# Gated expert rows added straight to the output in memory, with the closing pass taken out

## The chip, the core and the metric

The kernel runs on one core of a Trainium2 chip. The core has five engines with a queue of instructions each: PE (TensorE, matrix products), DVE (VectorE), ACT (ScalarE), POOL (GpSimd) and SP (SyncE, which here only issues DMAs). They run side by side and wait for one another through semaphores. DMAs that SP issues and the indirect ones that POOL issues run on the same 16 DMA engines. The metric is the device time in microseconds (us); three runs of the kernel before took 547.4, 556.72 and 557.5 us (median 556.72).

## What is computed

Input: 16 batches of 256 tokens with 128 features, conditioning vectors `c` and weights. Cut to what matters:

```
mod = (silu(c) @ wmod).reshape(16, 6, 1, 128)       # sa, ca, ga, sb, cb, gb
ga, gb: sign kept, magnitude at least 0.25
x = x + ga * attention(layernorm(x) * (1 + ca) + sa)   # 16 heads, causal, clipped scores
h = layernorm(x) * (1 + cb) + sb
# feed-forward: each token goes to 2 of 8 experts
normed = rmsnorm(h) * norm_weight
w, idx = top_k(softmax(normed @ router), 2);  w = w / sum(w)
moe = sum over the 2 experts of w * (silu(normed @ Wg) * (normed @ Wu)) @ Wd
out = x + gb * (h + clip(alpha) * moe)
```

All data are float32.

## The kernel before

**Attention loop.** A software pipeline over the 16 batches (`schedule`, turns -3 to 18, two of them unrolled in a loop body). In turn i every engine runs its part (`emit`) for seven batches at once: `front` (projections) for batch i + 2, `attn` (scores, exponentials, clip) for i, `back` for i - 1, `norm` (second normalisation) for u = i - 2, `route` for q = i - 3, and so on. The order within a turn is written out by hand, engine by engine, and each engine runs its list strictly in that order.

SP's list in a turn: `load_bc` (modulation rows of batch i into `bc`, after POOL's residual add L1114 of batch i - 2, semaphore `base_ready`), `keys_out` and `queries_out` (L382 to L395: projected keys and queries of batch i + 2 to DRAM), then `stack` twice (L401: they come back stacked, four copies each, after the writes have landed). DVE's list: `route` first (ranks, the two gate weights L887 and L892, destinations L894 in the expert queues), then `clip` of the first scores (L863, L865), the normalised rows `h2` (L903), then the rest. ACT squares `h2` (L726), POOL takes the root and adds `h2` times a row to the residual in `xall` (L1114). After `route`, POOL scatters the rows in `pl` (128 normalised features, gate weight, row number: `PAYW` = 130 words) into the DRAM tensor `queue`, sorted by expert, by four indirect DMAs a batch (L1122).

**Change of stage.** DVE turns the counts into a table (`bi`): for each of 71 blocks of 128 rows its expert and its first row in `queue`. Blocks past the last one are dummies. SP pads the ends of the experts' queues (L425), reads table entries into registers (L431) and loads blocks into `xb`, 8 buffers (L437).

**Expert stage.** In `block_steps` PE transposes block n + 2 (L647), computes gate and up products of n + 1 (L640) and the down product of n - 1 (L654); ACT and DVE do the activation and product; DVE scales the result by the gate weight into `ysb`, 8 buffers (L1040). POOL scatters it to `ydram` (L1148), where each token has two rows of its own, so that no scatter touches another's rows. A buffer of `xb` is loaded again when its scatter has landed (`yscat`).

**Closing pass.** When all has landed, SP reads the two halves of `ydram` in 8 chunks (L460), DVE adds them (L1050) and multiplies by the modulation row `gb * alpha` (L1054), POOL adds the residual (L1157) and SP writes the output (L464).

## Time and profile before

| | us |
|---|---|
| runs (3) | 547.4, 556.72, 557.5 |
| profiled execution, its own time | 549.46 |
| its span, first to last instruction | 547.6 |
| PE busy / DVE / ACT / POOL | 403.5 / 312.4 / 269.0 / 252.6 |

The busy times overlap; they are sums over stages with different limits. The profile is of a single execution, whose time is 7 us under the median, so that a sum of durations from it stands against 549.46 and not against the median. Line numbers are those of the kernel before. In rows, `SPq` is SP issuing a DMA, `xN` a number of instructions, and what stands in brackets is the engine's idle time ahead of the row and what ended it.

### The profile page before, as it was taken

How to read it: one execution, taken by the hardware profiler on the slowest of the kernel's cores; microseconds unless marked ns; L12 is line 12 of the kernel's file. 1: busy time of each engine (PE TensorE's matmuls, PEld its weight loads, DVE VectorE, ACT ScalarE, POOL GpSimd, SP SyncE). 2: the span in 40 equal slices, each digit the busy share in tenths (PEclk: the TensorE clock that was granted, in tenths of full speed). 3: DMA queues.
4: the chain of work that ended last, by engine and by line, in shares of the span. 5: the costliest groups of instructions: out<-in, count | busy, mean ns of one | idle time of the engine just before them, and what ended most of it. 6: DMA issues, size and time to landing. Idle time of an engine off the chain costs nothing. (4 is left out here: it accounts for less than half of the span.)

```text
span 547.6 us, 12530 instructions
## 1 busy us (share of the span) xinstructions
PE 403.5 (74%) x3935; PEld 320.6 (59%) x3936; DVE 312.4 (57%) x976; ACT 269.0 (49%) x467; POOL 252.6 (46%) x306
## 2 busy tenths in 40 slices
PE   3568876976697697697678752199999999999400
PEld 1345554654464464465456432089999999999400
DVE  3428967667754755756666666235554554555284
ACT  1427755655555455456555542245656655565100
POOL 3103437435743643644573487314444444444453
PEclk9999978877966866868787775589999999999855
DMA  8367445445444434434543082332221122112194
GB/s 263 73 154 166 118 101 123 114 109 131 100 115 116 104 88 115 104 90 115 130 97 105 19 317 84 91 100 64 58 69 54 55 64 60 55 54 65 43 293 138
DMA packets 56002, 59.04 MB, mean 108 GB/s; under 512 B 7167, under 2 KB 48128, under 8 KB 55712
## 3 DMA queue, kind: packets, MB, share of 16 engines
q1 hardware_dynamic: 51648, 50.15, 35.3%
q0 software_dynamic: 4320, 8.47, 4.6%
q8 instruction: 18, 0.29, 0.2%
q14 instruction: 16, 0.13, 0.1%
HBM read 34.81 MB, written 24.23 MB: 108 GB/s over the span
## 5 line engine op out<-in xcount | busy, mean ns | idle before, releaser
L673 ACT ACTIVATE pt<-SC 128x1536 f32<-128x1536 f32 x64 | 92.8, 1451 | 103.5 <-PE SC L500 103.3
L863 DVE SCALAR_TENSOR_TENSOR pt<-pt,cst 128x1024 f32<-128x1024 f32 x64 | 79.6, 1243 | 64.8 <-ACT pt L673 64.7
L1148 POOL DMA_INDIRECT ydram<-ysb,xb x71 | 69.8, 982 | 97.6 <-DVE ysb L1040 96.3
L640 PE MATMUL SC<-xTs,wgu 128*128 128x128 f32 x852 | 110.1, 280 | 2.3 <-issue 1.3
L640 PEld LDWEIGHTS SC<-xTs,wgu 128*128 128x128 f32 x852 | 102.8, 195 | 4.1 <-issue 3.9
L500 PE MATMUL SC<-stq,stk 24*128 24x256 f32 (+1 forms) x1024 | 78.9, 435 | 10.9 <-DMA stq<-qdram 8.1
L1122 POOL DMA_INDIRECT queue<-pl,dest x64 | 77.7, 1215 | 18.0 <-issue 17.2
L500 PEld LDWEIGHTS SC<-stq,stk 24*128 24x128 f32 x1024 | 59.5, 240 | 28.6 <-DMA stq<-qdram 8.4
L777 ACT ACTIVATE wgu<-gu,ws 128x704 f32 x71 | 62.1, 875 | 19.5 <-issue 19.5
L522 PE MATMUL OB<-pt,va 128*32 128x256 f32 (+1 forms) x1024 | 68.1, 394 | 3.3 <-DVE pt L865 3.2
L784 ACT ACTIVATE sg<-SC 128x384 f32<-128x384 f32 x71 | 34.8, 490 | 59.6 <-PE SC L640 53.8
L1034 DVE TENSOR_TENSOR hidT<-sg,SC 128x384 f32<-128x384 f32 x71 | 39.3, 554 | 31.4 <-PE FB L654 16.0
L1104 POOL TENSOR_TENSOR gbh<-h,bc 128x128 f32<-128x128 f32 x32 | 15.1, 493 | 78.7 <-DVE h L903 78.7
L522 PEld LDWEIGHTS OB<-pt,va 128*32 128x32 f32 x1024 | 30.5, 126 | 33.4 <-issue 19.6
L532 PE MATMUL FB<-tot,ut_bf 128*128 128x8 bf16 x16 | 2.9, 183 | 58.5 <-DVE tot L976 58.5
L532 PEld LDWEIGHTS FB<-tot,ut_bf 128*128 128x128 bf16 x16 | 1.6, 99 | 62.4 <-DVE tot L976 62.4
L654 PE MATMUL FB<-dn,hidT 128*128 x216 | 30.1, 275 | 0.5 <-DVE ysb L1040 0.5
L865 DVE TENSOR_SCALAR pt<-pt 128x512 f32<-128x512 f32 x64 | 30.3, 474 | 0.0
L1070 POOL TENSOR_TENSOR rstd<-var,mhalf 128x8 f32<-128x8 f32 x4 | 8.4, 2103 | 47.0 <-DVE var L812 47.0
L910 DVE TENSOR_TENSOR rope<-FB,cst 76x512 f32<-76x512 f32 x16 | 11.0, 685 | 33.2 <-PE FB L561 33.2
L1029 DVE COPY xTs<-OB 128x128 f32<-128x128 f32 x36 | 10.5, 291 | 33.5 <-PE OB L647 33.5
L654 PE MATMUL BK<-dn,hidT 128*128 x210 | 29.3, 275 | 0.0
(150 smaller groups left out, 654.3 us busy)
## 6 DMA issues: line engine op xcount, KB each, us to landing
stk<-kdram SPq DMA_DIRECT2D x64, 96.0 KB
stq<-qdram SPq DMA_DIRECT2D x64, 96.0 KB
xb<-queue SPq DMA_DIRECT2D x71, 65.0 KB, 1.8
kdram<-rope SPq DMA_DIRECT2D x32, 128.0 KB
qdram<-rope SPq DMA_DIRECT2D x32, 128.0 KB, 3.8
bc<-modrow SPq DMA_DIRECT2D x16, 256.0 KB
pt<-ydram SPq DMA_DIRECT2D x16, 256.0 KB, 5.3
gu<-gup SPq DMA_DIRECT2D x1, 2816.0 KB, 12.1
```

Source lines behind the costliest of these rows:

```text
L500: last = mm(SC[:, i, kt * S:S + kt * P], stk[at_, par(a), j, kt * P:(kt + 1) * P], stq[at_, par(a), j, kt * P:S], start=True, stop=True)
L522: last = mm(OB[VW * i:VW * i + VW, g * S + kt * P:(g + 1) * S], va[:, par(a), kt, n * VW:(n + 1) * VW], pt[:, j, i, kt * S:S + kt * P], st ...
L640: last = mm(GUB[b[1] % 2][:, n, c * P:(c + 1) * P], wgu[:, b[1] % 2, n, c * P:(c + 1) * P], xTs[:, b[1] % 2, :], start=True, stop=True)
L654: last = mm(YP[b[1] % 2][:, 0:D], hidT[:, b[1] % 2, n * P:(n + 1) * P], dn[:, bass.ds(e * (3 * D) + n * D, D)], start=(n == 0), stop=(n == 2))
L673: af(pt[:, j, :, 0:S + P], SC[:, :, 0:S + P], ACT.Exp, scale=SCALE).then_inc(s["exp_done"], 1)
L777: af(wgu[:, b[1] % 2, :, 0:HID], gu[:, bass.ds(expert(b) * (2 * HID), 2 * HID)].rearrange("p (n h) -> p n h", n=2), ACT.Copy, scale=ws[:, ...
L784: af(sg[:, b[1] % 2, :], GUB[b[1] % 2][:, 0, 0:HW], ACT.Silu).then_inc(s["sg_ready"], 1)
L863: stt(out=diag, in0=diag, scalar=E_LO, in1=mask, op0=ALU.max, op1=ALU.min)
L865: ts(off, off, E_LO, E_HI, ALU.max, ALU.min).then_inc(s["clip_done"], 1)
L1034: tt(hidT[:, b[1] % 2, :], sg[:, b[1] % 2, :], GUB[b[1] % 2][:, 1, 0:HW], ALU.mult)\
L1122: G.indirect_dma_start(queue, bass.IndirectOffsetOnAxis(dest[:, par(q), 2 * t + k:2 * t + k + 1], 0), pl[:, par(q), t, k, :], None).then_i ...
L1148: G.indirect_dma_start(ydram, bass.IndirectOffsetOnAxis(xb[:, slot(b), D + 1:D + 2].bitcast(u32), 0), ysb[:, slot(b), :], None, bounds_che ...
```

## The change

Each expert row now carries its modulation row with it, and goes by an accumulating scatter straight to the row of its token in the output tensor.

- In the attention loop SP, at the end of its part of a turn, copies the modulation row of batch i - 2 next to the normalised rows in `pl` (`gate_rows`; rows become 258 words), and the residual rows of that batch to the output (`rows_out`). DVE's second gate value waits for the first of these copies.
- `queue` gets 8 dummy blocks, written at the start; POOL writes zeros to 128 spare rows behind the output.
- DVE multiplies by both gate weight and modulation row. It also writes, for each block, how far the scatters of the block before it and of the one two before it must have come: up to that one itself where the expert differs, else only up to that buffer's previous use.
- POOL reads these numbers into registers, 16 for eight blocks, waits for them and for the scatter three blocks back, and issues the scatter with an addition.
- The closing pass is gone. `xTs`, `sg`, `hidT` and `ysb` lie in the space of `pt`.

```diff
@@ -59,12 +59,12 @@
...
+XBUF = 8
-PAYW = D + 2
+PAYW = 2 * D + 2
...
@@ -97,8 +100,7 @@
...
-    queue = nc.dram_tensor("queue", [(DUMMY + 1) * P, PAYW], fp32).ap()
-    ydram = nc.dram_tensor("ydram", [2 * NTOK, D], fp32).ap()
+    queue = nc.dram_tensor("queue", [(DUMMY + XBUF) * P, PAYW], fp32).ap()
...
@@ -273,26 +274,25 @@
...
-        bi = sb("bi", [1, 2, NBLK], i32)
+        bi = sb("bi", [1, 4, NBLK], i32)
...
@@ -363,7 +363,10 @@
...
             sp.dma_start(modrow, mrow[:, :]).then_inc(s["modrow_out"], DMA)
             sp.wait_ge(s["cst_in"], DMA)
-            sp.dma_start(queue[DUMMY * P:(DUMMY + 1) * P, :], cst[:, C_PAD:C_PAD + PAYW]).then_inc(s["dummy_out"], DMA)
+            for n in range(XBUF):
+                sp.dma_start(queue[(DUMMY + n) * P:(DUMMY + n + 1) * P, :], cst[:, C_PAD:C_PAD + PAYW])\
+                  .then_inc(s["dummy_out"], DMA)
+            out_rows = out.rearrange("(n p) d -> p n d", p=P)
             sp.wait_ge(s["modrow_out"], DMA)
...
@@ -401,6 +404,18 @@
...
+            def rows_out(u):
+                need(sp, s["base_ready"], num(u) + 1)
+                sp.dma_start(out_rows[:, col(u, T), :],
+                             xall[:, xtile(u)].rearrange("p (t d) -> p t d", d=D)).then_inc(s["rows_out"], DMA)
+            def gate_rows(u):
+                need(sp, scat[par(u)], half(u) * (DMA * 4))
+                row = modrow[col(u), 4 * D:5 * D].rearrange("(o b) d -> o b d", o=1)
+                sp.dma_start(pl[:, par(u), :, :, D + 2:].rearrange("p t k d -> p (t k) d"),
+                             row.to_broadcast([P, 2 * T, D])).then_inc(gb_in[par(u)], DMA)
...
@@ -410,6 +425,15 @@
                     queries_out(f)
                     stack(kdram, stk, stk_in, "k_out", f)
                     stack(qdram, stq, stq_in, "q_out", f)
+                if peeled(i) == 1:
+                    sp.wait_ge(s["dummy_out"], XBUF * DMA)
+                    sp.dma_start(queue[DUMMY * P:(DUMMY + XBUF) * P, D + 1:D + 3].rearrange("(n p) o -> p n o", p=P),
+                                 cst[:, C_DID:C_DID + 2 * XBUF].rearrange("p (n o) -> p n o", o=2))\
+                      .then_inc(s["dummy_out"], DMA)
+                if norm:
+                    gate_rows(u)
+                    rows_out(u)
                 if peeled(i) == B - 1:
                     sp.dma_start(gu[:, :], gup).then_inc(s["w_in"], DMA)
                     sp.dma_start(dn[:, :], down).then_inc(s["w_in"], DMA)
@@ -429,42 +453,27 @@
...
                 _, rows = nc.values_load_multi_w_load_instructions(
-                    bi[0:1, 1, at], engines=[mybir.EngineType.SP], min_val=0, max_val=DUMMY * P)
+                    bi[0:1, 1, at], engines=[mybir.EngineType.SP], min_val=0, max_val=(DUMMY + XBUF - 1) * P)
...
                 for n, row in enumerate(rows):
                     b = plus(k, n)
-                    need(sp, yscat[slot(b)], uses(b) * DMA)
+                    need(sp, yscat[slot(b)], (uses(b) + 1) * DMA)
                     sp.dma_start(xb[:, slot(b), :], queue[bass.ds(row, P), :]).then_inc(xb_in[slot(b)], DMA)
...
-                sp.wait_ge(s["dummy_out"], DMA)
+                sp.wait_ge(s["dummy_out"], (XBUF + 1) * DMA)
                 sp.wait_ge(s["padded"], E * DMA)
...
             load((0, 0), UNR2, queues_written)
-            sp.wait_ge(s["pv_done"], 4 * B)
...
             with sp.Fori(1, M1) as m:
                 load((m, 0), UNR2)
             load((M1, 0), NBLK - M1 * UNR2)
             for n in range(XBUF):
-                sp.wait_ge(yscat[n], (NBLK - n + XBUF - 1) // XBUF * DMA)
...
+                sp.wait_ge(yscat[n], ((NBLK - n + XBUF - 1) // XBUF + 1) * DMA)
         @block.tensor
@@ -889,6 +898,7 @@
                     V.tensor_reduce(destf[:, :], pd[:, :, :, :].rearrange("p t k e -> p (t k) e"), AX.X, ALU.add)\
                         .then_inc(s["destf_ready"], 1)
                     need(dve, s["c0_ready"], num(q) + 1)
+                    need(dve, gb_in[par(q)], (half(q) + 1) * DMA)
                     tt(pl[:, par(q), :, 1, D], ex[:, par(q), :], pl[:, par(q), :, 0, D], ALU.mult)
                     need(dve, s["destf_ready"], num(q) + 1)
                     cp(dest[:, par(q), :], destf[:, :]).then_inc(s["dest_ready"], 1)
@@ -1014,11 +1024,20 @@
...
-            chain(ts(bf_[:, 2, :], bf_[:, 1, :], -1.0, float(DUMMY), ALU.mult, ALU.add))
+            chain(tt(bf_[:, 2, :], cst[0:1, C_DUM:C_DUM + NBLK], bf_[:, 1, :], ALU.subtract))
...
             ts(bi[:, 1, :], bf_[:, 1, :], float(P), None, ALU.mult).then_inc(s["table_ready"], 1)
+            V.memset(bh[:, 1:3, 0:2], 0.0)
+            chain(tt(bh[:, 0, :], bf_[:, 0, :], ge[:, :, NE1], ALU.add))
+            tt(bh[:, 1, 1:NBLK], bh[:, 0, 1:NBLK], bh[:, 0, 0:NBLK - 1], ALU.is_gt)
+            chain(tt(bh[:, 2, 2:NBLK], bh[:, 0, 2:NBLK], bh[:, 0, 0:NBLK - 2], ALU.is_gt))
+            for n in range(2):
+                stt(out=bi[:, 2 + n, :], in0=bh[:, 1 + n, :], scalar=float(DMA),
+                    in1=cst[0:1, C_USE + n * NBLK:C_USE + (n + 1) * NBLK], op0=ALU.mult, op1=ALU.add).then_inc(s["order_ready"], 1)
...
@@ -1036,23 +1055,12 @@
...
                     b = plus(k, -1)
                     need(dve, s["y_done"], nb_(b) + 1)
-                    need(dve, yscat[slot(b)], uses(b) * DMA)
-                    ts(ysb[:, slot(b), :], YP[b[1] % 2][:, 0:D], xb[:, slot(b), D:D + 1], None, ALU.mult)\
+                    need(dve, yscat[slot(b)], (uses(b) + 1) * DMA)
+                    stt(out=ysb[:, slot(b), :], in0=YP[b[1] % 2][:, 0:D], scalar=xb[:, slot(b), D:D + 1],
+                        in1=xb[:, slot(b), D + 2:2 * D + 2], op0=ALU.mult, op1=ALU.mult)\
                         .then_inc(s["y_ready"], 1)
             block_steps(dve, step)
-            dve.wait_ge(s["gba_in"], DMA)
...
         @block.gpsimd
@@ -1073,6 +1081,13 @@
...
             finish_stats(0)
+            pool.wait_ge(s["cst_in"], DMA)
+            for n in range(XBUF):
+                part = slice(n * (P // XBUF), (n + 1) * (P // XBUF))
+                pool.dma_start(out[NTOK + n * (P // XBUF):NTOK + (n + 1) * (P // XBUF), :], cst[part, C_PAD:C_PAD + D])\
+                    .then_inc(yscat[n], DMA)
...
@@ -1135,26 +1150,44 @@
             G = nc.gpsimd
-            below = G.to_reg(2 * NTOK - 2)
-            bound = pool.alloc_register("bound")
-            def step(k, x, g, d):
-                if not d:
-                    return
-                b = plus(k, -1)
+            pool.wait_ge(s["rows_out"], B * DMA)
+            below, bound = G.to_reg(NTOK + (XBUF + 1) * P - 2), pool.alloc_register("bound")
+            def landed(k, count):
+                at = slice(nb_(k), nb_(k) + count) if isinstance(k[0], int) else bass.ds(k[0] * UNR2, count)
+                counts = []
+                for n in range(2):
+                    apart(pool)
+                    _, row = nc.values_load_multi_w_load_instructions(
+                        bi[0:1, 2 + n, at], engines=[mybir.EngineType.Pool],
+                        min_val=DMA, max_val=DMA * (NBLK // XBUF + 2))
+                    counts.append(row)
+                return list(zip(*counts))
+            def add_rows(b, before):
+                in_loop = not isinstance(b[0], int)
                 need(pool, s["y_ready"], nb_(b) + 1)
+                if in_loop or nb_(b) >= 3:
+                    need(pool, yscat[slot(plus(b, -3))], (uses(plus(b, -3)) + 2) * DMA)
+                for n in range(2):
+                    if in_loop or nb_(b) >= n + 1:
+                        pool.wait_ge(yscat[slot(plus(b, -1 - n))], before[n])
                 pool.reg_add(bound, below, 1)
-                G.indirect_dma_start(ydram, bass.IndirectOffsetOnAxis(xb[:, slot(b), D + 1:D + 2].bitcast(u32), 0),
-                                     ysb[:, slot(b), :], None, bounds_check=bound, oob_is_err=False)\
+                G.indirect_dma_start(out, bass.IndirectOffsetOnAxis(xb[:, slot(b), D + 1:D + 2].bitcast(u32), 0),
+                                     ysb[:, slot(b), :], None, bounds_check=bound, compute_op=ALU.add)\
                  .then_inc(yscat[slot(b)], DMA)
-            block_steps(pool, step)
-            pool.wait_ge(s["base_ready"], B)
...
+            pool.wait_ge(s["order_ready"], 2)
+            for n, before in enumerate(landed((0, 0), UNR2)):
+                add_rows((0, n), before)
+            with pool.Fori(1, M1) as m:
+                for n, before in enumerate(landed((m, 0), UNR2)):
+                    add_rows((m, n), before)
+            for n, before in enumerate(landed((M1, 0), NBLK - M1 * UNR2)):
+                add_rows((0, M1 * UNR2 + n), before)
@@ -1179,9 +1212,15 @@
     for t in range(T):
         for k in range(2):
             for b in range(B):
-                c[:, C_IDS + 2 * (T * b + t) + k] = (k * NTOK + b * S + t * P + p).astype(np.int32).view(np.float32)
+                c[:, C_IDS + 2 * (T * b + t) + k] = (b * S + t * P + p).astype(np.int32).view(np.float32)
     c[:, C_BLK:C_BLK + NBLK] = np.arange(NBLK)
-    c[:, C_PAD + D + 1] = np.full(P, PADID, np.int32).view(np.float32)
+    for n in range(2):
+        c[:, C_USE + n * NBLK:C_USE + (n + 1) * NBLK] = \
+            (np.maximum(np.arange(NBLK) - 1 - n, 0) // XBUF + 1) * 16
...
@@ -1223,7 +1262,7 @@
...
-    out = nc.dram_tensor("out", (B, S, D), mybir.dt.float32, kind="ExternalOutput").ap()
+    out = nc.dram_tensor("out", (NTOK + (XBUF + 1) * P, D), mybir.dt.float32, kind="ExternalOutput").ap()
...
-    return r.results[0]["out"]
+    return r.results[0]["out"][0:NTOK].reshape(B, S, D)
```

The instruction streams show where this stands. SP, one turn of the loop, before (`L401` are the stack loads, `L372` the modulation rows of the next turn):

```order
L401 DMA stk<-kdram 24x1024 [waits k_out]
L401 DMA stk<-kdram 24x1024 x3
L401 DMA stq<-qdram 24x1024 [waits q_out]
L401 DMA stq<-qdram 24x1024 x3
L372 ISA [waits base_ready,cst_in]
L372 DMA bc<-modrow 128x512
```

and of the change (`L404`, `L375` are the same lines):

```order
L404 DMA stq<-qdram 24x1024 [waits q_out]
L404 DMA stq<-qdram 24x1024 x3
L211 ISA
L416 ISA [waits scat0]
L416 DMA pl<-modrow 128x4x128
L410 ISA [waits base_ready]
L410 DMA out<-xall 128x2x128
L375 ISA [waits base_ready,cst_in]
```

Two copies stand between a turn's stack loads and the next turn. DVE, at the top of the next turn, of the change:

```order
L896 RECIPROCAL pl<-den 128x2 [waits den_ready,pl_ready]
L898 TENSOR_REDUCE destf<-pd 128x4 [waits pd_ready]
L902 TENSOR_TENSOR pl<-ex,pl 128x2 [waits gb_in1,c0_ready]
L904 CAST dest<-destf 128x4 [waits destf_ready]
L872 SCALAR_TENSOR_TENSOR pt<-pt,cst 128x8x128 [waits exp_done]
L874 TENSOR_SCALAR pt<-pt 128x4x128
L913 SCALAR_TENSOR_TENSOR h<-t,rstd,bc 128x128 [waits pl_ready,gbh_ready,rstd2_ready,t1_ready]
```

The order is that of before; new is the wait for `gb_in1` at L902 (L892 before), ahead of the clip and of the normalised rows. POOL, at the top of a group of eight blocks in the expert stage, of the change (before, each scatter has one wait, `y_ready`, and one register instruction):

```order
L1163 TENSOR_LOAD bi
L1163 ISA x16
L1163 ISA [waits cst_in]
L1178 REGISTER_ALU [waits yscat6,yscat7,yscat5]
L1179 DMA out<-pt,xb 5248x128
L1178 REGISTER_ALU [waits yscat0,yscat7,yscat6,y_ready]
```

The first two rows stand there twice, one load for each of the two counts; then the scatters follow with their waits for the three before them.

## Rows read from the trace of the kernel before

**Rows 1.** Windows: stretch, length, busy us of each engine, granted clock, DMA share.

```profile
70.00:160.00 90.00, 68.84 (x761) 47.24 (x761) 59.72 (x197) 51.32 (x95) 46.01 (x62) 0.77 0.46 115
...
440.00:515.00 75.00, 72.13 (x635) 71.18 (x633) 37.38 (x102) 41.37 (x65) 34.52 (x36) 1.00 0.20 56
...
515.00:548.00 33.00, 0.00 (x0) 0.00 (x0) 17.09 (x24) 0.00 (x0) 13.40 (x10) 0.54 0.71 191
```

**Rows 2.** Chain of waits, its end: start us, us, what.

```profile
514.04 0.98 POOL ydram L1148
...
515.32 2.09 DMA ydram<-ysb,xb
...
517.56 0.38 SPq L460
```

**Rows 3.** Timeline of SP: start us, us, engine, line, operation.

```profile
16.81 0.42 SPq L366 DMA_DIRECT2D queue<-cst  x1
...
81.27 1.58 SPq L401 DMA_DIRECT2D stq<-qdram  x4
...
152.70 1.51 SPq L401 DMA_DIRECT2D stq<-qdram  x4
```

**Rows 4.** Timeline of DVE: gate value L892, clip L863, normalised rows L903.

```profile
76.17 0.15 DVE L892 TENSOR_TENSOR pl<-ex,pl 128x2 f32<-128x2 f32 x1
...
134.53 1.23 DVE L863 SCALAR_TENSOR_TENSOR pt<-pt,cst 128x1024 f32<-128x1024 f32 x1 [1.98 <-ACT pt L673]
...
136.00 0.61 DVE L903 SCALAR_TENSOR_TENSOR h<-t,rstd,bc 128x128 f32<-128x128 f32 x2
...
150.01 0.15 DVE L892 TENSOR_TENSOR pl<-ex,pl 128x2 f32<-128x2 f32 x1
...
289.83 0.15 DVE L892 TENSOR_TENSOR pl<-ex,pl 128x2 f32<-128x2 f32 x1
```

**Rows 5.** Timeline of ACT and POOL in the same turn.

```profile
137.90 0.31 ACT L726 ACTIVATE sqj<-h 128x128 f32<-128x128 f32 x1
...
140.68 0.73 POOL L1114 TENSOR_TENSOR xall<-xall,gbh 128x256 f32 x1
```

**Rows 6.** Timeline of the start: POOL, SP and PE.

```profile
25.03 1.64 POOL L1070 TENSOR_TENSOR rstd<-var,mhalf 128x8 f32<-128x8 f32 x1 [13.74 <-DVE var L812]
...
27.60 1.58 SPq L401 DMA_DIRECT2D stq<-qdram  x4
...
31.89 1.66 PE L500 MATMUL SC<-stq,stk 24*128 24x256 f32 x16 [8.15 <-DMA stq<-qdram]
```

**Rows 7.** DMA issues: what, count, KB each, median us to landing.

```profile
xb<-queue SPq DMA_DIRECT2D x71, 65.0 KB, 1.8
...
stq<-modrow SPq DMA_DIRECT2D x1, 1024.0 KB, 5.4
...
dn<-down SPq DMA_DIRECT2D x1, 1536.0 KB, 15.3
```

**Rows 8.** Timeline of the expert stage: POOL, SP and PE.

```profile
376.15 0.98 POOL L1148 DMA_INDIRECT ydram<-ysb,xb  x1 [1.14 <-DVE ysb L1040]
...
378.74 0.33 SPq L437 DMA_DIRECT2D xb<-queue  x1
...
508.10 0.27 PE L647 MATMUL OB<-cst,xb 128*128 128x128 f32 x1
...
508.62 0.98 POOL L1148 DMA_INDIRECT ydram<-ysb,xb  x1 [1.14 <-DVE ysb L1040]
```

**Rows 9.** Chain of waits, 378 to 392 us.

```profile
384.91 1.71 SPq L431
...
388.70 0.04 SPq L209
```

**Rows 10.** Timeline of the change of stage: SP and DVE.

```profile
316.40 0.42 SPq L415 DMA_DIRECT2D dn<-down  x1
...
334.03 0.15 DVE L892 TENSOR_TENSOR pl<-ex,pl 128x2 f32<-128x2 f32 x1
```

59 lines of the change are left out of this document (17 added, 42 removed).

## The prediction

> **What bounds the kernel now.** I read the windows by stage first. From 70 to 160 us, the attention loop, no engine is full (PE 69 of 90 us, POOL 46); from 440 to 515 us, the expert stage, PE is full (72 of 75 us at clock 1.00); from 515 us on PE does nothing [rows 1]. So the second stage is bound by PE, the closing pass by itself, and the loop by a cycle of waits. Then the chain: the last scatter of expert rows has landed when SP issues its first read of them at 517.56 us, and everything to 547.6 us is the closing pass [rows 2]. Then SP's own rows in the loop, because the change puts copies into that queue. One turn of SP is released by the residual add on POOL (140.68 plus 0.73 us) and ends with four loads of stacked queries, issued by 152.70 + 1.51 = 154.21 us [rows 3, 5]. Turns follow one another at 18 to 20.5 us: the sixteen writes of the second gate value on DVE go from 76.17 us (batch 0) to 289.83 us (batch 11), 19.4 us each on average [rows 4].
>
> **The closing pass, removed.** 547.6 - 517.5 = 30.1 us, all on the path [rows 2]: **-30.1**.
>
> **The gated rows, added to SP's queue.** Before, DVE had what it needed at the gate value of batch 5, say. Now it waits there for a copy that spreads a modulation row over `pl`; SP issues this copy at the end of the turn before, behind all key and query copies. What each side reaches: SP is through with the stacks of the turn that holds batch 0 at 81.27 + 1.58 = 82.85 us, DVE was at that value at 76.17; for a later batch it is 154.21 against 150.01 us [rows 3, 4]. The copy is late by its place in the queue, whatever its own price. Behind DVE's wait stand the clip of the next scores, the second normalisation and the gate arithmetic of all following work; PE waits for the clip, POOL for the normalised rows, and SP's next turn for POOL. So the wait closes a cycle, and its length becomes the period:
> - DVE from the copy's landing to the normalised rows: 0.3 us for two small instructions, then the clip and its companion, 136.00 - 134.53 = 1.5 us; ACT's exponentials are done by then, so its 1.98 us of waiting falls away [rows 4]. 1.8 us.
> - From there to the residual add's end: 141.41 - 136.00 = 5.4 us, less 1.1 us for which ACT was held (its square began at 137.90 us, the rows were ready at 136.61) [rows 4, 5]. 4.3 us.
> - SP's turn: 154.21 - 141.41 = 12.8 us [rows 3, 5]. Rows scattered by POOL in that time double in width, which can hold up SP's copies: I take 13.1.
> - The copy: not in this trace in this form. The last stack load of the start was issued by 29.18 us and PE began at 31.89: 2.7 us, which the new copy has ahead of it [rows 6]. A copy of 1024 KB of the same kind takes 5.4 us and one of 65 KB 1.8 [rows 7], so 256 KB adds about 1 us: 3.7. Ends: 2.7 (hidden in the drain) and 2.7 + 5.4 = 8.1.
>
> Period 1.8 + 4.3 + 13.1 + 3.7 = 22.9 us. The turns that hold key and query copies are followed by 12 such waits (batches 0 to 11). Start: eight block-wide copies to the queue's dummy blocks, 0.42 us each to issue, stand before the first key copy instead of one [rows 3]: 2.9 us, and 1 MB of writes in front of the keys: +3 (ends 2 and 6). The first wait ends at 82.85 + 3 + 3.7 = 89.6 us, the twelfth at 89.6 + 11 x 22.9 = 341.5, against 289.83 before: +51.7, less the 1.9 us that ACT is ahead: **+50**. Ends: with 20.5 us a turn +24, with 25 us +73. The last copies have no stacks ahead of them, but one comes behind the expert weights, which land at 316.40 + 15.3 = 331.7 us, with DVE at its value at 334.03 [rows 7, 10]: in time, by 1 to 2 us.
>
> **The expert stage.** Now PE takes 2.12 us a block, and a block is transposed 0.52 us before the block four earlier is scattered (508.10, block 70; 508.62, block 66) [rows 8]. A scatter's buffer is free for SP 378.74 - 376.15 = 2.6 us after its start [rows 8], 2.1 at the end of the stage [rows 2]; the load that follows takes 1.8 [rows 7]. Two things are added on POOL.
> - Before each group of eight scatters POOL reads 16 wait counts from memory into registers, in two loads of eight. SP does one such load: 1.71 us for the memory read and 16 register instructions behind it, 3.9 us from 384.8 to 388.7 [rows 9]. Two make 7.8 us in POOL's queue, between two scatters that now start 2.12 us apart (and 1.28 at least, 514.04 to 515.32 [rows 2]). Nothing hides it: the buffers run out. The cycle of one group: 1.28 + 7.8 us to the next scatter, its landing, 1.8 us load, 0.5 us to the scatter four on, 3 x 2.12 to the last of the group.
> - The accumulating scatter: no row shows one. It must read what it adds to; a read of 65 KB takes 1.8 us in all [rows 7]. Ends 0 and 1.8 more than the plain 2.6; I take 0.8, as the fixed part overlaps: 3.4 us.
>
> Group: 9.1 + 3.4 + 1.8 + 0.5 + 6.4 = 21.2 us, against 17.4 now (8 x 2.12 and 0.45 us that PE waits at SP's load). 8 such groups: 8 x 3.8 = 30 us. At each of up to eight changes of expert a scatter starts 3.4 us after the last instead of 1.28; about a third of these 8 x 2.1 us falls on the cycle: 6 us. **+36**. Ends: with one load hidden (3.9 us) the cycle is 17.3 us and the changes alone count, +6; with a landing of 3.6 + 1.8 = 5.4 us it is 8 x 5.8 + 11 = +57.
>
> A rule to weigh: the memory read in such a register load shows 1.71 us [rows 9]. The Trainium skill, DMA: Bandwidth & Descriptors, section on latency and other measured facts, gives a floor of about 600 ns for it. With that, two loads would be 5.4 us, the cycle 18.8, the stage +17 and the sum 587 by an estimate; this trace disagrees.
>
> **Small edits.** Rows and loads twice as wide at the change of stage: +1 (ends 0 and 3). POOL's eight zero copies at the start, at 1.28 us each, lie in 13.74 us of idle time before 25.03 us [rows 6]; without that cover they cost 10. DVE's added table instructions lie beside SP's 3.9 us of register loads. The output rows written in the loop stand behind the gated rows in SP's queue and need an add that is already done: 0. DVE multiplies by two factors in one pass instead of one, and is not the bound: 0.
>
> **Sum**: 549.46 (profiled execution) - 30.1 + 50 + 36 + 1 = **606 us**. The median of the three runs shown is 556.72, 7 us above that execution, so 606 is 9% over the median.
>
> **The rivals.** What a measurement of this kernel tells from no change is about 2%, 546 to 568 us.
> - *POOL's register loads are cheaper than SP's*: one of the two memory reads costs nothing, 7.8 - 1.7 = 6.1 us. Group of 19.5 us, the stage 8 x 2.1 + 6 = +23: 593 us. For it: POOL is another engine; against: the same instructions in one queue. 0.12. The skill's floor for the read, above, would do the same to both reads.
> - *Landing dominates*: the accumulating scatters take 5.4 us, or PE, which now stops in each group, is granted 1.2 instead of 2.4 GHz as in the loop (0.77 on average there [rows 1]), and itself becomes the bound. 549.5 - 30.1 + 50 + 57 + 1 = 627 us. 0.16.
> - *Both cycles close near their low ends*: 549.5 - 30.1 + 24 + 6 + 1 = 550 us, no change. It needs the copy hidden in the drain and one register load hidden. 0.06.
> - *Faster*: the gated rows are there in time. It decides at DVE's gate value: the copy must land 4.2 us before SP's last stack load is issued (150.01 against 154.21), so it would have to overtake the stack loads, which only SP's order rules out. Then 549.5 - 30.1 + 3 + 6 + 1 = 529 us. 0.04.
> - *The scatters do wait for one another*: a scatter always waits for the one three earlier, so from 3 x 2.12 = 6.4 us of landing on the relaxed order saves nothing; at 7.5 us the stage is 70 x (2.5 - 2.12) = 27 us longer by that alone, besides the loads: some 640 us. 0.03.
>
> The forecast has 0.59. Range: from 572 (the loop at 20.5 us a turn and the group at 20 us) to 640; it leaves out the two cases below 568 and the far end of the landing. Slower by over 2%: 0.59 + 0.12 + 0.16 + 0.03 = 0.90; within 2%: 0.06; faster: 0.04.
>
> **What would show it.** In the profile of the changed kernel: DVE idle 3 to 8 us (13 at the first) before the second gate value of batches 0 to 11, released by the copy `pl<-modrow`; turns of 22 to 24 us; a granted clock in the loop no higher than now; POOL's table lines of some 8 us between the eighth and the ninth scatter and PE idle for 3 to 4 us once a group, released by the loads of `xb`; from the last scatter to the end 3 to 5 us. I am wrong if DVE doesn't wait there, or if PE runs through the expert stage at 2.12 us a block.

## The result and the profile after

The changed kernel takes **705.5 us** (median of four runs, 705.05 to 707.13), the kernel before 557.1 in the same comparison (547.4 to 559.9): 1.282 times as long, 95% interval 1.270 to 1.295. The forecast was 606, with a range up to 640. The sign was right, the time 100 us too short. The profiled execution took 707.13 us, its span is 705.3. Between the two spans (547.6 and 705.3) lie 157.7 us, and three marks in the traces divide them:

| stage | before | after | difference | predicted |
|---|---|---|---|---|
| start to the first scatter of expert rows | 365.6 | 491.9 | +126.3 | +51 |
| first to last of the 71 scatters | 149.7 | 206.9 | +57.2 | +36 |
| from the last scatter to the end | 32.3 | 6.5 | -25.8 | -30.1 |

Windows of the kernel after: stretch, length, busy us of PE, PEld, DVE, ACT and POOL, granted clock, DMA share, GB/s.

```profile
70.00:160.00 90.00, 53.23 (x522) 36.46 (x523) 39.35 (x127) 34.74 (x66) 31.05 (x44) 0.71 0.36 92
96.00:400.00 304.00, 197.77 (x1763) 132.91 (x1763) 131.24 (x440) 118.12 (x216) 107.83 (x143) 0.65 0.40 100
492.00:700.00 208.00, 163.85 (x1286) 160.48 (x1285) 75.39 (x204) 86.04 (x133) 110.14 (x71) 0.87 0.40 63
```

Against [rows 1] every engine is less busy in the loop (PE 53 of 90 us instead of 69) and the clock is lower. In the expert stage PE, which was full, now works 164 of 208 us.

**The loop.** DVE at the second gate value, which is now L902, in the kernel after:

```profile
96.79 0.16 DVE L902 TENSOR_TENSOR pl<-ex,pl 128x2 f32<-128x2 f32 x1 [14.47 <-DMA pl<-modrow]
...
125.03 0.17 DVE L902 TENSOR_TENSOR pl<-ex,pl 128x2 f32<-128x2 f32 x1 [12.89 <-DMA pl<-modrow]
...
153.57 0.16 DVE L902 TENSOR_TENSOR pl<-ex,pl 128x2 f32<-128x2 f32 x1 [11.83 <-DMA pl<-modrow]
...
405.01 0.16 DVE L902 TENSOR_TENSOR pl<-ex,pl 128x2 f32<-128x2 f32 x1 [12.82 <-DMA pl<-modrow]
```

DVE stands there 9.8 to 14.5 us in each of these twelve turns, behind the copy of the modulation row. The twelfth wait ends at 405.0 us; before, DVE was there at 289.8 [rows 4]. The eleven turns between take (405.0 - 96.8) / 11 = 28.0 us each, against 19.4. Now one turn of SP, the residual add on POOL, and the chain of waits at the copy:

```profile
143.04 1.51 SPq L404 DMA_DIRECT2D stq<-qdram  x4
144.86 0.41 SPq L416 DMA_DIRECT2D pl<-modrow  x1
145.59 0.44 SPq L410 DMA_DIRECT2D out<-xall  x1
159.75 0.36 SPq L375 DMA_DIRECT2D bc<-modrow  x1
...
172.21 1.51 SPq L404 DMA_DIRECT2D stq<-qdram  x4
173.94 0.41 SPq L416 DMA_DIRECT2D pl<-modrow  x1
```

```profile
158.79 0.73 POOL L1129 TENSOR_TENSOR xall<-xall,gbh 128x256 f32 x1
```

```profile
144.86 8.62 DMA pl<-modrow
```

The cycle is the one that the forecast named: copy, gate value, normalised rows, residual add, SP's turn, copy. The stacks are issued by 144.55, the copy has landed when DVE goes on at 153.57 (9.0 us), the residual add ends 5.95 us later, and SP has issued the next stacks 14.2 us after that: 29.2 us for this turn.

**The change of stage.** Chain of waits of the kernel after, batches 13 and 14:

```profile
434.52 15.36 DMA queue<-pl,dest
...
449.89 9.60 DMA pl<-modrow
```

The row scatters of batch 12 stand behind the two loads of expert weights (gate and up weights now take 17.5 us to land, down weights 22.1; down was 15.3 [rows 7]), and the copy into the same buffer cannot be issued before they have landed. The gate value of batch 14 comes at 459.58 us instead of 334.03 [rows 10]: the lag, 115 us so far, grows to 125.6 there.

**The expert stage.** The scatters on POOL (L1179) in one group of eight:

```profile
564.19 1.56 POOL L1179 DMA_INDIRECT out<-pt,xb  x1 [7.33 <-issue]
...
577.11 1.56 POOL L1179 DMA_INDIRECT out<-pt,xb  x1 [1.95 <-DMA out<-pt,xb]
579.23 1.55 POOL L1179 DMA_INDIRECT out<-pt,xb  x1 [0.56 <-issue]
588.14 1.56 POOL L1179 DMA_INDIRECT out<-pt,xb  x1 [7.36 <-issue]
```

and the chain of waits through the same group:

```profile
564.19 3.42 DMA out<-pt,xb
567.77 2.22 DMA xb<-queue
570.03 0.47 PE OB L656
570.51 1.39 PE BK L663 x6
571.90 2.56 PE SC L649 x12
...
579.54 1.84 POOLq L1163
581.41 0.15 POOLq L1163
...
583.35 1.83 POOLq L1163
...
588.14 3.25 DMA out<-pt,xb
591.56 2.02 DMA xb<-queue
...
595.48 2.56 PE SC L649 x12
```

A group lasts 588.14 - 564.19 = 23.95 us. In it stand the two memory reads for the wait counts (1.84 and 1.83 us) with their checks of 0.15 us a value. POOL needs 1.56 us to issue an accumulating scatter, where the plain one took 0.98 [rows 8]; that alone costs nothing, since PE needs 2.12 a block. And PE, after it has stood still, does twelve products (L649) in 2.56 us. Windows of these two stretches, of a later one in the group, and of the kernel before in its expert stage (columns as above):

```profile
571.90:574.40 2.50, 2.50 (x13) 2.50 (x13) 0.82 (x2) 0.00 (x0) 2.11 (x2) 0.50 0.78 106
595.40:598.00 2.60, 2.60 (x13) 2.34 (x11) 0.82 (x2) 0.00 (x0) 1.99 (x3) 0.50 0.48 76
583.00:588.00 5.00, 5.00 (x47) 5.00 (x46) 2.51 (x7) 3.25 (x7) 0.00 (x0) 1.00 0.09 26
```

```profile
500.00:512.00 12.00, 11.72 (x106) 11.53 (x104) 6.31 (x18) 5.95 (x10) 5.89 (x6) 1.00 0.13 40
```

The granted clock is 0.50 after the stop (1.2 GHz) and 1.00 again at the end of the group; before, it was 1.00 all the time, and the twelve products took 1.34 us, six down products 0.67:

```profile
506.92 1.34 PE SC L640 x12
...
508.37 0.67 PE BK L654 x6
```

From the page of the kernel after, its costliest groups (idle time and its releaser at the end) and its DMA issues:

```profile
L1179 POOL DMA_INDIRECT out<-pt,xb x71 | 110.6, 1558 | 115.3 <-issue 75.4
...
L902 DVE TENSOR_TENSOR pl<-ex,pl 128x2 f32<-128x2 f32 x16 | 2.6, 162 | 153.9 <-DMA pl<-modrow 153.9
...
xb<-queue SPq DMA_DIRECT2D x71, 129.0 KB, 2.2
...
pl<-modrow SPq DMA_DIRECT2D x16, 256.0 KB, 8.5
```

The end: the last scatter starts at 698.78 us, 6.5 us before the end of the span.

### The profile page after: what moved, and what is told of

The parts are those of the page before. It is cut to its first block, busy times and chain, and to the rows that moved or that the text cites. A ratio compares the mean times of both kernels' runs of the same rounds, so it can differ in the third digit from the quotient of the medians.

```text
span 705.3 us, 13062 instructions
## 1 busy us (share of the span) xinstructions
PE 455.7 (65%) x3935; PEld 358.0 (51%) x3936; DVE 293.3 (42%) x958; ACT 270.6 (38%) x467; POOL 281.0 (40%) x307
## 4 chain that ended last, share of the span: by engine, by line
DMA 32%; issue 17%; PE 16%; SPq 10%; POOLq 8%; POOL 7%; DVE 6%; ACT 2%; DVEq 0%; ACTq 0%
DMA pl<-modrow 13%; POOLq L1163 7%; DMA out<-pt,xb 7%; DMA qdram<-rope 5%; PE SC L509 4%; SPq L398 4%; POOL out L1179 4%; PE OB L531 3%; DMA queue<-pl,dest 3%; SPq L404 3%; PE SC L649 2%; DMA kdram<-rope 2%; ACT pt L682 1%; DMA xb<-queue 1%; PE FB L589 1%
## 5 line engine op out<-in xcount | busy, mean ns | idle before, releaser
L1179 POOL DMA_INDIRECT out<-pt,xb x71 | 110.6, 1558 | 115.3 <-issue 75.4
L649 PE MATMUL SC<-pt,wgu 128*128 128x128 f32 x852 | 117.5, 293 | 2.5 <-DVE pt L1053 1.0
L649 PEld LDWEIGHTS SC<-pt,wgu 128*128 128x128 f32 x852 | 110.8, 208 | 3.8 <-issue 2.5
L509 PE MATMUL SC<-stq,stk 24*128 24x256 f32 (+1 forms) x1024 | 88.8, 481 | 14.2 <-DMA stq<-qdram 11.5
L793 ACT ACTIVATE pt<-SC 128x384 f32<-128x384 f32 x71 | 34.8, 490 | 108.3 <-PE SC L649 108.0
L1137 POOL DMA_INDIRECT queue<-pl,dest x64 | 65.9, 1030 | 18.0 <-issue 16.9
L902 DVE TENSOR_TENSOR pl<-ex,pl 128x2 f32<-128x2 f32 x16 | 2.6, 162 | 153.9 <-DMA pl<-modrow 153.9
L1053 DVE TENSOR_TENSOR pt<-pt,SC 128x384 f32<-128x384 f32 x71 | 39.4, 554 | 38.6 <-PE BK L663 20.0
L656 PE MATMUL OB<-cst,xb 128*128 128x128 f32 x36 | 11.5, 319 | 47.3 <-DMA xb<-queue 47.3
L1048 DVE COPY pt<-OB 128x128 f32<-128x128 f32 x36 | 10.5, 292 | 66.3 <-PE OB L656 66.3
L663 PE MATMUL BK<-dn,pt 128*128 x210 | 34.6, 309 | 0.0
L663 PE MATMUL FB<-dn,pt 128*128 x216 | 32.3, 289 | 0.5 <-DVE pt L1059 0.5
## 6 DMA issues: line engine op xcount, KB each, us to landing
gu<-gup SPq DMA_DIRECT2D x1, 2816.0 KB, 17.5
```

The source lines that it names most:

```text
L509: last = mm(SC[:, i, kt * S:S + kt * P], stk[at_, par(a), j, kt * P:(kt + 1) * P], stq[at_, par(a), j, kt * P:S], start=True, stop=True)
L649: last = mm(GUB[b[1] % 2][:, n, c * P:(c + 1) * P], wgu[:, b[1] % 2, n, c * P:(c + 1) * P], xTs[:, b[1] % 2, :], start=True, stop=True)
L663: last = mm(YP[b[1] % 2][:, 0:D], hidT[:, b[1] % 2, n * P:(n + 1) * P], dn[:, bass.ds(e * (3 * D) + n * D, D)], start=(n == 0), stop=(n == 2))
L793: af(sg[:, b[1] % 2, :], GUB[b[1] % 2][:, 0, 0:HW], ACT.Silu).then_inc(s["sg_ready"], 1)
L1053: tt(hidT[:, b[1] % 2, :], sg[:, b[1] % 2, :], GUB[b[1] % 2][:, 1, 0:HW], ALU.mult)\
L1137: G.indirect_dma_start(queue, bass.IndirectOffsetOnAxis(dest[:, par(q), 2 * t + k:2 * t + k + 1], 0), pl[:, par(q), t, k, :], None).then_i ...
```

## Experiments

The kernel before takes 557 us (547 to 560) on the chip of the result. On those of the experiments it took 580 (one run), 572 (564 to 585) and 569 (563 to 588). So stages are compared inside traces (first gate value to sixteenth; first scatter to last), and times only with runs from the same chip. One unchanged kernel showed 149.7 and 151.9 us for the expert stage in two traces, so 2 us there are no effect. Version 8 and the early spreading have four runs each, all others one.

**1. The copy's place in SP's queue.** Its price stays, its place changes:

```diff
                 if attn:
                     load_bc(a)
+                if norm:
+                    gate_rows(u)
                 if front:
                     keys_out(f)
...
-                if norm:
-                    gate_rows(u)
```

> The changed kernel, with the copy of the gated rows moved to the head of SP's part of a turn, right behind the modulation rows; nothing else. The copy takes 8.6 us to land at the end of the turn, DVE reaches its second gate value about 8.6 us after the residual add. If the place in SP's queue is what closes the cycle, DVE's waits at L902 (153.9 us in all) shrink to under 25 us and the turns go from 28.0 to 19 to 21 us, the kernel to 600 to 625 us. If the copy's own length is what counts wherever it stands, or if the key copies behind it are pushed back by as much, turns stay above 25 us and the kernel above 670 us.

Measured: 609.8 us, 98 us less than with the copy at the end (707.6 on the same chip, experiment 3). The page of this kernel gives the copy the same 8.5 us to landing, but now they pass beside SP's key copies. DVE waits 14.5 us in all, not 154, and the expert stage is as long as in the changed kernel (206.6 us). The first scatter starts at 394.9 us, in the changed kernel at 491.9. So nearly 100 of the 126 us of the first stage are the wait at the end of SP's turn. The turns are (305.7 - 86.2) / 11 = 20.0 us; all of this is as expected.

**2. What the copy reads.** The same bytes into the same place, but from 128 different rows of 2 KB instead of 512 times the same 512 bytes:

```diff
-                row = modrow[col(u), 4 * D:5 * D].rearrange("(o b) d -> o b d", o=1)
+                row = gup[:, 0:2 * T * D].rearrange("p (n d) -> p n d", d=D)
```

> The changed kernel, with the copy of the gated rows reading 128 different rows of 2 KB of a weight tensor instead of one row of 512 bytes 512 times; same bytes, same descriptors' size, same place; the gates are wrong by this. If the single source row makes the copy slow (8.6 us from issue to landing), it lands in 3 to 4.5 us and the 12 turns are 4 to 5 us shorter each: 645 to 655 us. If not, 700 to 706 us.

**3. Where the copy writes.** Gate weight and row number moved behind the two rows of 128 words, the row in `pl` padded to 272 words, so that each 512-byte piece of the copy starts on a 64-byte boundary:

```diff
+PLW = 2 * D + 16
-        pl = sb("pl", [P, 2, T, 2, PAYW])
+        pl = sb("pl", [P, 2, T, 2, PLW])
...
-                sp.dma_start(pl[:, par(u), :, :, D + 2:]...
+                sp.dma_start(pl[:, par(u), :, :, D:2 * D]...
```

> The changed kernel, with the gated rows at a word offset of 128 in rows of 272 words in SBUF (before: offset 130 in rows of 258), so that each 512-byte piece begins on a 64-byte boundary; the rows scattered stay 258 words. If the destination's alignment makes the copy slow, it lands in 3 to 4.5 us and the kernel takes 645 to 655 us. If not, 700 to 706 us.

Measured: 640.8 us with other source rows (4 us under what was expected; its gates are not those of the task), 707.6 with the aligned target (2 over). The target makes no difference: the copy lands in 8.4 us and the wait totals 130.5 us. The source does. SP and DVE of the kernel with other source rows, one turn:

```profile
204.38 1.51 SPq L404 DMA_DIRECT2D stq<-qdram  x4
205.94 0.41 SPq L416 DMA_DIRECT2D pl<-gup  x1
```

```profile
209.62 0.16 DVE L902 TENSOR_TENSOR pl<-ex,pl 128x2 f32<-128x2 f32 x1 [9.68 <-DMA pl<-gup]
...
232.64 0.16 DVE L902 TENSOR_TENSOR pl<-ex,pl 128x2 f32<-128x2 f32 x1 [4.76 <-DMA pl<-gup]
```

From the last stack load's issue (205.89) to the gate value 3.7 us pass in this turn, the term that the forecast took for this copy; all waits sum to 82.7 us. Turns come down from (467.4 - 97.4) / 15 = 24.7 us (aligned, all fifteen) to (400.3 - 92.4) / 15 = 20.5. So the copy is slow because of its source, one row of 512 bytes read 512 times. As far as the packets of the profile tell, the pieces are no smaller than with the other source: this line of the changed kernel is, but for the mean rate (108 GB/s), that of the kernel with other rows too:

```profile
DMA packets 65347, 69.07 MB, mean 98 GB/s; under 512 B 8464, under 2 KB 57488, under 8 KB 65056
```

Reading a single row is not slow by itself either. The modulation rows of each turn (`bc<-modrow`, also 256 KB) come from one row of 2 KB that is read 128 times, and in the kernel before POOL waited once for them:

```profile
70.65 0.36 SPq L372 DMA_DIRECT2D bc<-modrow  x1
...
73.99 0.45 POOL L1099 TENSOR_TENSOR wog<-ws,bc 128x128 f32<-128x128 f32 x1 [1.17 <-DMA bc<-modrow]
```

They had landed 3.3 us after the issue began (3.5 in the changed kernel). And the load of 1024 KB from sixteen rows, 5.4 us before [rows 7], read each row in pieces of 512 bytes 128 times. Slow is only the copy that has both, small pieces and one row for all 512 of them. Why is not shown.

**4. The expert stage without loads and waits.** Each token gets two output rows, so no scatter can meet another; POOL's loads of counts and its waits for scatters are gone. It prices the stage and is no replacement:

```diff
-                if in_loop or nb_(b) >= 3:
-                    need(pool, yscat[slot(plus(b, -3))], (uses(plus(b, -3)) + 2) * DMA)
-                for n in range(2):
-                    if in_loop or nb_(b) >= n + 1:
-                        pool.wait_ge(yscat[slot(plus(b, -1 - n))], before[n])
...
-            for n, before in enumerate(landed((0, 0), UNR2)):
+            for n, before in enumerate([None] * UNR2):
...
-  ... = (b * S + t * P + p).astype(np.int32).view(np.float32)
+  ... = (k * NTOK + b * S + t * P + p).astype(np.int32).view(np.float32)
```

> The changed kernel, with the two expert rows of a token added to rows of their own in an output of twice the rows, so that no scatter needs to wait for another, and with the waits and POOL's register loads left out; the output is not summed by this. It prices the accumulating scatter alone. If the loads and waits lengthen the expert stage (206.9 us from first to last scatter, against 149.7 before), it falls to 150 to 153 us and the kernel to 650 us. If the accumulating scatters are slow by themselves (1.56 us of POOL each, 3.3 us to landing), the stage stays above 170 us and the kernel above 668 us.

Measured: 659.6 us, the stage 156.1 us, a little over the 150 to 153 expected and far under 170. On POOL:

```profile
569.00 1.55 POOL L1174 DMA_INDIRECT out<-pt,xb  x1 [0.56 <-issue]
571.11 1.56 POOL L1174 DMA_INDIRECT out<-pt,xb  x1 [0.55 <-issue]
...
575.35 1.56 POOL L1174 DMA_INDIRECT out<-pt,xb  x1 [0.56 <-issue]
578.51 1.55 POOL L1174 DMA_INDIRECT out<-pt,xb  x1 [1.60 <-DVE pt L1059]
```

Scatters 2.12 us apart, with accumulation: PE's pace of before. Of the 57 us that the stage gained, 50.8 are loads and waits. The other 6.4 are what accumulation and wider rows cost at most, since 2 us of it can be the difference between chips.

**5. The loads without the waits.** As the last, with the loads back, and counts that never ask for more than a buffer's previous use:

```diff
-                stt(out=bi[:, 2 + n, :], in0=bh[:, 1 + n, :], scalar=float(DMA),
+                stt(out=bi[:, 2 + n, :], in0=bh[:, 1 + n, :], scalar=0.0,
```

> As the run with rows of their own for both expert rows of a token, but with POOL's register loads of 16 counts per group of eight blocks kept, and waits that ask only for what has long landed; the output is not summed by this. Of the 50.8 us by which that run shortened the expert stage (206.9 to 156.1 us from first to last scatter), the loads should take back 30 to 38 us, to 186 to 194 us (8 groups of 7.3 us of load that the buffers don't cover), and the waits at the changes of expert the rest. If the waits are what costs, the stage stays under 165 us.

Measured: 700.1 us, the stage 201.3 us. Against experiment 4 the loads cost 45.2 us, more than the 30 to 38 expected, and against the changed kernel all waits for other scatters only 5.6 us. The rival in which scatters wait for one another is out. The seventh scatter of a group in this run, and the first of the next:

```profile
551.54 1.56 POOL L1177 DMA_INDIRECT out<-pt,xb  x1 [2.21 <-DMA out<-pt,xb]
...
562.44 1.56 POOL L1177 DMA_INDIRECT out<-pt,xb  x1 [7.23 <-DVE pt L1059]
```

The gap of some 2 us before the seventh (577.11 us in the changed kernel) stands here too, at the same place in four groups (2.1 to 2.2 us), although no scatter waits for a recent one. So it is no wait for a scatter, whatever the row names: DVE's result (L1059) is what comes late. The groups last 24.0 us (562.44 to 586.43), as in the changed kernel.

**6. One load instead of two.** The scatter two blocks back is always waited for, by a constant, and only one count a block comes from the table:

```diff
-                for n in range(2):
-                    apart(pool)
-                    _, row = nc.values_load_multi_w_load_instructions(
-                        bi[0:1, 2 + n, at], engines=[mybir.EngineType.Pool],
+                apart(pool)
+                _, rows = nc.values_load_multi_w_load_instructions(
+                    bi[0:1, 2, at], engines=[mybir.EngineType.Pool],
...
-                if in_loop or nb_(b) >= 3:
-                    need(pool, yscat[slot(plus(b, -3))], (uses(plus(b, -3)) + 2) * DMA)
+                if in_loop or nb_(b) >= 2:
+                    need(pool, yscat[slot(plus(b, -2))], (uses(plus(b, -2)) + 2) * DMA)
```

> The changed kernel with one count per block instead of two: POOL always waits for the scatter two blocks back, by a constant, and by a count from memory only for the one before; half the loads, 3.7 us a group instead of 7.3. The stage falls from 206.9 to 170 to 182 us and the kernel to 670 to 682 us. If a scatter's landing (3.3 us) is what fills the group, the wait two blocks back costs more than it saves and the stage stays above 195 us.

Measured: 684.0 us, the stage 183.4 us, both just outside what was expected. POOL of this kernel:

```profile
570.65 1.56 POOL L1175 DMA_INDIRECT out<-pt,xb  x1 [0.30 <-issue]
575.39 1.56 POOL L1175 DMA_INDIRECT out<-pt,xb  x1 [3.18 <-issue]
579.49 1.55 POOL L1175 DMA_INDIRECT out<-pt,xb  x1 [2.54 <-DMA out<-pt,xb]
```

The stall is 3.2 us here (3.0 to 3.5 in the other groups) instead of 7.3. Leaving one load out is worth 206.9 - 183.4 = 23.5 us, about half of the 45.2 that both cost, and that is with a wait for the scatter two blocks back added: the second load is no cheaper than the first.

**7. The row spread on chip.** `bc` holds the modulation row too, and POOL writes it into `pl`; SP's copy and DVE's wait are gone:

```diff
-                src = modrow[col(a), 0:4 * D].to_broadcast([P, 4 * D])
+                src = modrow[col(a), 0:5 * D].to_broadcast([P, 5 * D])
...
-                if norm:
-                    gate_rows(u)
...
-                    need(dve, gb_in[par(q)], (half(q) + 1) * DMA)
...
                     last.then_inc(s["gbh_ready"], 1)
+                    G.tensor_copy(pl[:, par(u), :, :, D + 2:].rearrange("p t k d -> p (t k) d"),
+                                  bc[:, par(u):par(u) + 1, 4 * D:5 * D].to_broadcast([P, 2 * T, D]))\
+                        .then_inc(s["gb_ready"], 1)
```

> The changed kernel, with the modulation row put beside the normalised rows by a POOL copy from the rows that already lie in SBUF (the copy bc<-modrow gets 640 words wide instead of 512) instead of a DMA; DVE's wait for it is gone. With the DMA and the cycle through it gone, turns are 19 to 20.5 us and the first expert scatter starts at 370 to 385 us instead of 491.9; the kernel takes 585 to 600 us. If the loop is long for another reason (output rows written in it, scattered rows twice as wide), turns stay above 23 us and the kernel above 640 us.

Measured: 602.6 us (700.1 and 684.0 with the copy, on the same chip). The spreading takes 0.61 us a turn on POOL. Gate values 82.3 to 364.9 us, first scatter at 391.0: 6 us past the end of what was expected (370 to 385), 25 later than in the kernel before on the chip of the result.

**8. All three together**: spread on chip, one load, and the dummy blocks written inside the loop, after its first turns, instead of ahead of it.

```diff
-            for n in range(XBUF):
-                sp.dma_start(queue[(DUMMY + n) * P:(DUMMY + n + 1) * P, :], ...
...
                 if peeled(i) == 1:
+                    for n in range(XBUF):
+                        sp.dma_start(queue[(DUMMY + n) * P:(DUMMY + n + 1) * P, :], ...
+                if peeled(i) == 3:
                     sp.wait_ge(s["dummy_out"], XBUF * DMA)
```

> On-chip modulation rows, one count per block, and the eight dummy blocks written after the first turns instead of ahead of the first key copies. The three gains add up if their causes are separate: 705 - 115 - 30 - 4 = 556 us, between 545 and 565, no different from the kernel before by 2%; faster than before only if the expert stage falls below 165 us.

Measured: 583.2 us, 1.027 times the kernel before (1.013 to 1.040), so slower by an amount that may lie on either side of 2%. The expectation missed by 18 us: the expert stage is 183.2 us as in 6, but the first scatter again starts at 391.1. Writing the dummy blocks later brought 2 us at the first gate value (80.3 instead of 82.3) and none at the first scatter.

**9 to 12. Where the last 25 us of the loop are**, on one more chip: the kernel before again; version 8 with the spreading ahead of POOL's wait for the normalised rows; the latter without the residual rows; and the latter with queue rows of 130 words.

> The kernel before, unchanged, traced on this chip: it tells apart what differs by chip and what by kernel. If the 19 us that the loop of the last combined version has more than the kernel before (from the first to the sixteenth gate value 284.3 us against 263.6) belong to the chip, this run too shows 275 us or more there and a span over 560 us. If they belong to the kernel, it shows 262 to 266 us, and 150 us from the first to the last scatter of the expert stage.

> The combined version (modulation row spread on POOL, one count a block, dummy blocks late), with POOL's spreading moved ahead of its wait for the normalised rows, where POOL has 6.6 us of idle time in each turn. Theory A (the spreading, 0.6 us, and its neighbours lie on the cycle through the residual add): turns get 0.6 to 0.9 us shorter, the first expert scatter starts 8 to 12 us earlier, near 380. Theory B (the wider rows and the residual rows on the DMA engines lengthen the turn): no change, 389 to 392. Either way the time stays over that of the kernel before on the same chip, since the expert stage keeps its 183 us.

```diff
# copy_early, against 8
                     need(pool, scat[par(u)], half(u) * (DMA * 4))
+                    G.tensor_tensor(pl[:, par(u), :, :, D + 2:]..., gate_row, nothing, ALU.add)
                     need(pool, s["h2_ready"], num(u) + 1)
...
-                    G.tensor_copy(pl[:, par(u), :, :, D + 2:]...
# no_rows, against copy_early
-                if norm:
-                    rows_out(u)
# narrow, against copy_early
-    queue = nc.dram_tensor("queue", [(DUMMY + XBUF) * P, PAYW], fp32).ap()
+    queue = nc.dram_tensor("queue", [(DUMMY + XBUF) * P, ROWW], fp32).ap()     # ROWW = D + 2
...
-                                pl[:, par(q), t, k, :], None).then_inc(scat[par(q)], DMA)
+                                pl[:, par(q), t, k, 0:ROWW], None).then_inc(scat[par(q)], DMA)
```

> As the run with the early spreading, and the copies of the residual rows to the output (128 KB a turn from SP) left out, so that only the expert rows are in the output. Theory B for these copies: a copy that SP issues at the end of its turn delays the key copies and row scatters behind it, 0.5 us a turn or more, first gate value to sixteenth at least 7 us shorter than with them. Otherwise within 3 us.

> As the run with the early spreading, but the rows in the queues are 130 words again, as before the change, and the modulation factors in the expert stage are ones, so that the gating by gb is left out. Theory B for the doubled rows: four scatters of 66 instead of 132 KB a turn and half the bytes in each load of a block; first gate value to sixteenth 8 to 15 us shorter, the expert stage 0 to 8 us shorter than 183. If the width costs nothing, both stay within 3 us.

| | time | first to 16th gate value | expert stage |
|---|---|---|---|
| kernel before, first chip | 549.5 | 263.7 | 149.7 |
| kernel before, this chip | 565.6 | 277.6 | 151.9 |
| early spreading | 589.7 (583.1 to 605.9) | 290.1 | 183.9 |
| and no residual rows | 616.0 | 317.9 | 182.4 |
| and narrow rows | 587.8 | 290.4 | 181.9 |

The second gate value of the version without residual rows (in the kernel before on this chip, at the same place, 197.03, 217.48 and 238.00, so 20.5 us a turn):

```profile
217.25 0.15 DVE L890 TENSOR_TENSOR pl<-ex,pl 128x2 f32<-128x2 f32 x1
...
241.17 0.15 DVE L890 TENSOR_TENSOR pl<-ex,pl 128x2 f32<-128x2 f32 x1
```

Three things follow. First, the unchanged kernel shows 277.6 us here. Version 8 had 284.3, which is 20.6 us over 263.7 (the expectation says 19), and 14 of them are within what one kernel shows between two executions on two chips. That is the second case of the expectation (275 or more). But not all of it is the chip: here, on one chip, the version with the early spreading still has 12.5 us more in the loop than the kernel before (290.1 against 277.6), and its first scatter starts at 398.2 us instead of 379.5. Second, no gain from the spreading's place shows. Neither theory had 398.2 us (near 380, or 389 to 392), and version 8 itself did not run on this chip. POOL did not have the 6.6 us: in the window 200 to 300 us the early instruction waited 16.4 us, in five waits, for the row scatters that last read the buffer. Third, fewer bytes don't help: narrow rows change neither stage, and with the residual rows left out the turn is 23.9 us, longer than with them (neither of the two cases expected). That last isn't a cost of leaving a transfer out that I can explain; in the window 200 to 300 us ACT waits 19.3 us for something that the trace doesn't name, 2.9 in the version with the residual rows. What sets a turn between 17 and 24 us once DVE doesn't wait for the copy stays open.

Of these versions the one with the early spreading alone keeps the whole computation; it is 1.037 times the kernel before (1.019 to 1.056). No version beats the kernel before.

## Why the prediction was right in sign and 100 us short

**The closing pass.** Right in kind: 30.1 us predicted, 25.8 measured. The same stretch before, from the last scatter on, was 32.3 us, and now 6.5 follow instead of the 3 to 5 that were said.

**The wait at the gate value.** The place, the cause and the cycle were right: DVE waits for `pl<-modrow` in each turn, and DVE's part and that to the residual add came to 5.95 us (6.1 predicted). What failed is the term for the copy: "so 256 KB adds about 1 us: 3.7", with its far end at 8.1. It measured 9.0. It was scaled by bytes from loads whose source rows are many; this copy reads one row for all its 512 pieces. Experiment 2 shows that by bytes the term was right: 3.7 us where the source is other rows. No load in the trace of before combines one row with pieces of 512 bytes; the nearest in bytes, `bc<-modrow`, took 3.3 us, close to the 3.7 (experiment 3). With SP's turn at 14.2 instead of 13.1, a turn is 28.0 us against 22.9. Over eleven turns that is 56 us, and the first wait ends at 96.8 us instead of 89.6, 7 us more (5.0 from the copy, 2.3 because SP's stack loads come later): 63 us of the miss. The 1.9 us that ACT was to win back did not show: the lag was 115.2 us at the twelfth wait and 126.3 at the first scatter. "DVE idle 3 to 8 us" was wrong by the same 5 us and more, since the longer cycle leaves DVE idle through all of SP's turn; "turns of 22 to 24 us" too. "A granted clock in the loop no higher than now" held: 0.71 from 70 to 160 us against 0.77 [rows 1], and 0.65 from 96 to 400 us.

**The last copies.** "In time, by 1 to 2 us" failed, and that is a second wrong step. The forecast looked at when the weights land in the trace of before, but not at what the added bytes do in that traffic, and not at the row scatters, which the next copy has to wait for. DVE waits 1.4 us at the gate value of batch 13 and 8.0 at that of batch 14, and the lag of the loop grows by 10 us there. With the copy at the head of SP's turn (experiment 1) DVE still waits 7.5 us at batch 14.

**The expert stage.** The cycle was right, and three of its four terms fit, in the group from 564.19 us:

| term | predicted | measured |
|---|---|---|
| eighth scatter to the first of the next group | 9.1 | 8.9 |
| its landing | 3.4 | 3.4 |
| load of the buffer, with its issue | 1.8 | 2.4 |
| from there to the eighth scatter | 6.9 | 9.2 |
| group | 21.2 | 23.95 |

The memory read of the loads: the Trainium skill, DMA: Bandwidth & Descriptors, section on latency and other measured facts, gives a floor of about 600 ns. On POOL a read for eight values shows 1.83 us, on SP 1.71 [rows 9]. That is three times the floor, which doesn't contradict it; but the floor can't stand for the price of such a read, and the rival of cheaper loads went with it (experiment 6: one load less is worth 23.5 us). By the forecast's own numbers two loads at that floor come to 7.8 - 2.2 = 5.6 us, not 5.4.

The mis-sized term is the last: after its stop PE needs more than 2.12 us a block. The transposition of the block just loaded takes 0.47 us instead of 0.11, six down products 1.39 instead of 0.67 and the twelve products 2.56 instead of 1.34, together 2.3 us (granted clock 0.50 there, 0.87 over the stage, 1.00 before). The row of the seventh scatter names another scatter as what ended its wait, but it starts 0.79 us after DVE's result, as the eighth does, and the same gap stands in the run without such waits (experiment 5). So it is PE's own pace after the stop, and no wait for a scatter, that makes up the 2.3 us. A group is 2.75 us longer than predicted, and eight of them 22 us, which covers the 21 us that the stage missed. The lower clock was named in the second half of the rival "Landing dominates". That its stage figure, +57, is the measured one is luck: it was worked out from a landing of 5.4 us, which did not come, and not from the clock. Its total of 627 us was still 78 short, since it kept the loop at +50. The waits at changes of expert were put at 6 us of path time and cost 5.6 by experiment 5.

**Small edits.** The eight dummy blocks and wider rows at the start: +3 predicted, the first residual add starts 5.9 us later (75.73 instead of 69.84). Inside the ends of 2 and 6.

**The range.** It ended at 640, short of the two far ends together. With both, the text's own numbers give 549.5 - 30.1 + 73 + 57 + 1 = 650, still 55 short: no end in it covered a source that is slower than any load of its size in the trace, and none covered the last copies being late.

## What to carry to other kernels

Before a copy is put in front of a busy engine's instruction, ask not only how many bytes it moves but from how many different rows and in what pieces, and price it by a load that matches in both. Here one row read 512 times in pieces of 512 bytes cost 8.5 us, and one row read 128 times in pieces of 2 KB 3.3. Where the row is on chip already, spread it there: that cost 0.6 us a turn. A late transfer in a loop whose stages feed one another is paid once per turn, so an error of 5 us in its landing became 60. Numbers that an engine must read into registers cost a memory read and a check each, at the worst place: they stop the queue, and then PE restarts at its lower clock.

## What the runs showed of the hardware

- A copy of 256 KB that reads one row of 512 bytes 512 times lands 8.4 to 8.6 us after its issue (medians of six kernels), whether or not its target pieces start on 64-byte boundaries (experiment 3). The same bytes from 128 rows of 2 KB take some 3.6 us, and from one row of 2 KB read 128 times 3.3 us.
- An accumulating indirect scatter of 128 rows of 512 bytes costs POOL 1.56 us to issue (plain: 0.98) and lands 3.3 us after its start (3.25 to 3.42 in the chain shown, medians of 3.3 to 3.6 in the other kernels). Accumulation itself did not slow the stage by more than 6.4 us in 71 scatters.
- Eight values read into registers take POOL some 3.7 us: 1.83 for the memory read, then a check of 0.15 every 0.23 us. Two such loads held up the first scatter of each full group by 7.3 to 7.5 us, one by 3.0 to 3.5.
- After the two stops shown the first twelve products took 2.56 us instead of 1.34, at a granted clock of 0.50.
- One unchanged kernel showed 263.7 and 277.6 us for the same loop on two chips, and its runs took 547 to 560 us on one chip and 563 to 588 on another, so a difference of a few per cent, between chips above all, says nothing about an edit.
